# A graph transformer layer on one core: the second half of each item's token products moves behind the next item's slice logits

## What is computed

```
h  = xn @ W.T + b;  a1 = h @ w_a1 + b_a1;  a2 = h @ w_a2 + b_a2
v  = leaky_relu(a1[row] + a2[col], 0.01)            # one score per edge
att = softmax of v over the edges of one row
gnn = segment_sum(att * h[col], row)
mix = linear attention (8 heads, feature map elu + 1) of xn, then @ wo + bo
x   = x + gnn + mix
y   = layernorm(x)
w   = softmax(((y @ W_x + b_x) @ W_slice + b_slice) / temperature)   # 8 heads x 64 slices per node
slice_token = sum over nodes of w * (y @ W_fx + b_fx), over the sum of w
x   = x + (attention among the 64 slice tokens of a head, spread back by w) @ W_out + b_out
```

## Time and profile before

| | us |
|---|---|
| median of 3 runs | 2304.6 |
| lowest, highest run | 2302.0, 2306.59 |
| span of the profiled execution (no other time of it is given) | 2306.1 |
| TensorE busy | 1454.6 |
| VectorE busy | 1270.9 |
| GpSimd busy | 1004.7 |
| ScalarE busy | 677.9 |
| mean granted TensorE clock (share of 2.4 GHz) | 0.798 |

### The profile page before, as it was taken

How to read it: one execution, slowest core, us unless ns; L and a number is a source line. 1 busy time by engine, 2 the same in 40 slices (tenths; PEclk the granted TensorE clock), 3 DMA queues, 4 the chain that set the end, 5 groups by cost and what they waited for, 6 DMA issues and landing times. The chain is left out here.

```text
span 2306.1 us, 27679 instructions
## 1 busy us (share of the span) xinstructions
PE 1454.6 (63%) x8420; PEld 1093.9 (47%) x8420; DVE 1270.9 (55%) x4043; ACT 677.9 (29%) x1884; POOL 1004.7 (44%) x1126
## 2 busy tenths in 40 slices
PE   5599995355745655655655656656646547465889
PEld 3477874234534434434434434434434435344667
DVE  8978783154644644644644545545545535445744
ACT  0243441042322322322322323323323323223310
POOL 1167676535445445445345345345344354453000
PEclk8799997577778877778878778778777777787999
DMA  8011213223223223223223222222232232221064
GB/s 178 29 47 48 62 50 90 71 58 88 70 70 87 69 69 86 69 73 84 68 73 83 68 76 80 68 77 79 65 83 77 62 87 68 69 77 55 14 193 153
DMA packets 112593, 177.17 MB, mean 77 GB/s; under 512 B 35998, under 2 KB 84509, under 8 KB 112445
## 3 DMA queue, kind: packets, MB, share of 16 engines
q0 software_dynamic: 43184, 109.96, 18.0%
q1 hardware_dynamic: 52847, 44.64, 7.5%
q10 hardware_dynamic: 16414, 20.81, 2.9%
HBM read 139.68 MB, written 35.65 MB: 76 GB/s over the span
## 5 line engine op out<-in xcount | busy, mean ns | idle before, releaser
L1134 POOL DMA_INDIRECT big<-node_table,rest x825 | 784.9, 951 | 239.9 <-issue 225.9
L1220 PE MATMUL psum<-big 128*125 128x257 f32 x1700 | 399.2, 388 | 39.4 <-DVE big L1757 39.1
L1220 PEld LDWEIGHTS psum<-big 128*125 128x125 f32 x1700 | 316.2, 191 | 93.9 <-DVE big L1757 46.1
L1575 DVE TENSOR_SCALAR rest<-psum,rest 128x125 f32<-128x125 f32 x100 | 30.1, 344 | 594.8 <-remote 554.1
L1239 PE MATMUL psum<-rest 65*125 65x512 bf16 x52 | 34.6, 666 | 488.6 <-ACT big L1376 488.6
L1132 POOL TENSOR_TENSOR rest<-rest 1x1 f32<-1x1 f32 x100 | 18.9, 189 | 693.7 <-PE psum L1220 668.0
L1370 ACT ACTIVATE rest<-big,rest 128x125 f32<-128x125 bf16 x850 | 268.9, 493 | 134.2 <-DVE rest L1705 134.2
L1239 PEld LDWEIGHTS psum<-rest 65*125 65x125 bf16 x52 | 9.2, 176 | 521.2 <-ACT big L1376 521.0
L1376 ACT COPY big<-psum 128x250 f32<-128x250 f32 x52 | 19.1, 367 | 687.1 <-remote 682.5
L1241 PE MATMUL psum<-rest,big 128*125 128x512 f32 x208 | 177.5, 1005 | 0.0
L1757 DVE TENSOR_SCALAR big<-big,rest 128x125 f32<-128x125 bf16 x850 | 169.0, 281 | 0.0
(11 more groups left out here) (430 smaller groups left out, 2786.7 us busy)
## 6 DMA issues: line engine op xcount, KB each, us to landing
big<-node_table,rest POOLq DMA_INDIRECT x825
slice_weights<-rest ACTq DMA_DIRECT2D x51, 252.0 KB
big<-slice_weights SPq DMA_DIRECT2D x50, 252.0 KB, 3.8
node_table<-big SPq DMA_DIRECT2D x50, 126.0 KB
normalised_turned<-big SPq DMA_DIRECT2D x50, 125.0 KB
rest<-normalised_turned SPq DMA_DIRECT2D x50, 125.0 KB
out_dram<-rest ACTq DMA_DIRECT2D x50, 125.0 KB
X<-in_x_dram SPq DMA_DIRECT2D x1, 5600.0 KB
```

The source lines that it names most:

```text
L1134: pool.indirect_dma_start(Gt[:, u, q * TW:(q + 1) * TW], None, table, bass.IndirectOffsetOnAxis(ap=item[:, u, 2 * q:2 * q + 1], axis=0)).t ...
L1220: mm = pe.matmul(bank[bAgg][0:R, 0:D + 1], P[:, u, q, :], Gt[:, at, q * TW:q * TW + D + 1], start=q == 0, stop=q == Q - 1)
```

## The change

In the gather loop `tokens` of a step is cut in two: the first half of y's columns stays where it was, and the second half is issued in the next step, directly behind that step's `logits`, from the y buffer of the item before; `sum_psum` is raised behind it. The very first step has none of a step before it; the final step first does the half of the item before and then its own two halves as before.

```diff
--- before.py
+++ after.py
@@ -1249,12 +1249,15 @@
                                            start=True, stop=True)
                         mm.then_inc(swT_psum, 1)
 
+                    def token_half(c, u, L=L, last=False):
+
+                        return pe.matmul(bank[bSum + c][:, :], y[:, u, c * 128:(c + 1) * 128], L, start=False, stop=last,
+                                         skip_group_check=True)
+
                     def tokens(n, u, L=L, last=False):
 
-                        for c in range(DC):
-                            mm = pe.matmul(bank[bSum + c][:, :], y[:, u, c * 128:(c + 1) * 128], L, start=False, stop=last,
-                                           skip_group_check=True)
-                        mm.then_inc(sum_psum, 1)
+                        token_half(0, u, L, last)
+                        token_half(1, u, L, last).then_inc(sum_psum, 1)
 
                     def queries(m, v, k):
 
@@ -1298,11 +1301,13 @@
                                            stop=c == DC - 1)
                         mm.then_inc(mix_psum, 1)
 
-                    def step(i, j, k, ahead, final=False):
+                    def step(i, j, k, ahead, final=False, first=False):
                         u, n, odd = j % U, 2 * k + j // U, j % 2
                         v, w, nv = (u + 1) % U, (u + 2) % U, n + 1 if u == U - 1 else n
                         spread(i)
                         logits(i)
+                        if not first:
+                            token_half(1, (u - 1) % U).then_inc(sum_psum, 1)
                         norms(i + 1)
                         if ahead:
                             turn(i + 1, v)
@@ -1319,7 +1324,7 @@
                             logits(i + 1, bF2, yT2)
                             tokens(i, u)
                             return
-                        tokens(i, u)
+                        token_half(0, u)
                         if ahead:
                             queries(i + 2, w, nv)
                         mix(i + 1)
@@ -1332,7 +1337,7 @@
                     turn(0, 0)
                     turn_largest(0)
                     for i in range(SURE):
-                        step(i, i % LU, i // LU, True)
+                        step(i, i % LU, i // LU, True, first=i == 0)
                     with pe.Fori(MIN_ROUNDS - 1, more) as k:
                         for j in range(LU):
                             step(LU * k + j, j, k, True)
```

## The result

| | before | after |
|---|---|---|
| median, us (7 runs each; before: the three runs above and four more) | 2302.0 | 2312.24 |
| lowest, highest | 2292.66, 2306.59 | 2311.38, 2314.56 |
| profiled execution, its span | 2306.1 | 2309.7 (time 2311.46) |
| mean granted TensorE clock, profiled execution | 0.798 | 0.793 |

The changed kernel is slower: the ratio of the times is 1.0046, with a 95% interval of 1.003 to 1.0063, or about 10 us. The forecast was 2321, 16.7 us above its base. The chips are called by letters: B, C and D are three different ones. On which chip this pair ran is not on record; it is called A. Its times before (2292.7 to 2306.6 us) do not overlap those of B and D (2279.7 to 2291.5 us), so it is probably a fourth.

The account below looks back on a forecast made before the run. The prediction took a ring of y copy, gather and delayed y transpose signal as the bound. Tail saving 0 plus 16.7 us of delay on 2306.1 gave 2322.8, on the median's scale 2321; range 2302 to 2340.

Parts of the forecast that it names:

- The ring: Gather loop step: y copy to first edge sums' end 10.83 us, marker and gather 20.15, until y transpose seen 3.16.
- the first piece: Gather loop step, from the y copy to the end of the first edge sums (POOL's marker): 10.83 us.
- Two records at 0.86 or 1.71 us: TensorE, directly behind the logits: the two moved matmul records take 0.86 us at full clock, 1.71 at half.
- The wait on VectorE: VectorE's subtraction waits for sum_psum behind the two records, delaying edge sums and gather: 0.78 us at clock 0.50, 16.7 in all.
- 49 windows: The 1.71 us from 4.31 us after each y copy, whose granted clock prices the records; 15 cost nothing.
- TensorE's room: TensorE's 0.84 us wait for VectorE ahead of the edge sums; 1.71 us more would make them 0.87 late.
- The tail worth nothing: TensorE's tail loses two records, 0.86 us a step, worth 0 because the y transpose's signal is used only after the gather.
- Hidden entirely: Rival: the two records last 0.86 us and fit VectorE's 1.18 us; no change, 2304.6 us, up to 2309; chance 0.17.
- Cold everywhere: Rival: the wait on sum_psum holds 0.78 us in nearly every step, 36 us more, 2341 us; chance 0.12.
- The tail counts: Rival: each matmul record in TensorE's tail costs while POOL gathers; two fewer give 50 us less, 2271 us; chance 0.12.

Follow-up runs that it names:

- half_ahead: Changed kernel with the moved half ahead of the logits, not behind them: 2284.87 us, ratio 0.9994 to the kernel before on chip B; 2284.63 us, 0.9987 on D.
- ring_vector_b: Kernel before, with VectorE's marks and first scores under the gather, weighings before the subtraction, ScalarE's transposes copy before its exponential: 2236.62 us (D); as ring_vector 1593.56 us (C).
- both_behind: Changed kernel with both halves of the token products behind the next step's logits, none in the tail: 2339.52 us, ratio 1.0225 to the kernel before, chip B.
- half_severed: Changed kernel, moved product reading constant weights, sum_psum raised by the tail's half, second half of token sum left out: 2283.54 us, ratio 0.9981 to before, chip B.
- narrowing: Changed kernel with the moved half on 256 of its 512 columns, the other 256 left out: 2284.43 us, ratio 0.9989 to the kernel before, chip B.

## Why the prediction was right, point by point

**The ring** held. In nearly every step of the profiles of chips A, B and D the order is copy, marker, gather, copy; the exceptions are the uneven steps from the 40th on, nine steps of half_ahead on chip B and every fourth of ring_vector_b. Undoing the load on the first piece takes the loss away (half_ahead), doubling it raises the loss (both_behind), and shortening that piece shortens the kernel (ring_vector_b).

**Two records at 0.86 or 1.71 us** held: 1.02 us with the last record's end at 2.4 GHz, 1.92 at 1.2 GHz, streaming 0.86 and 1.71 us.

**The wait on VectorE** held in mechanism and size. Forecast 0.78 us at PEclk 0.50, measured 0.89, of which 0.04 was there before (the start stands 6.34 us after the copy, 5.49 in the earlier trace rows); forecast 16.7 us over the loop, measured 18.5 on chip A and 16.1 on chip D. The marker moved by 0.36 and 0.33 us, forecast 0.35. The forecast had spread the cost over 34 of 49 windows with three sizes. On chip A it came in 19 steps nearly whole, and hardly at all in the others: the clock's rise comes back at the same places every four steps there (3.8, 4.0, 6.4 and 5.7 us after the copy in neighbouring steps), so a step is either mostly cold or not at all. That the sum over such other steps comes out the same is in part luck. The Trainium skill, "TensorE: Matmul & The Clock Gate" (The HAM clock gate), has a throttled state as the default that activity releases; the prediction took this rule, alone, to make the move free. The trace agrees with the release and not with a free move: on chip A it came 5.6 to 6.5 us after the copy in half of the steps, too late for two records that begin at 4.3.

**TensorE's room** of 0.84 us shrank as forecast (the edge sums' line waits 32.2 us for VectorE from 400 to 2050 us, and waited 71.1 us there before), but not to nothing: 0.55 us are left in a warm step. That it is the second bound and not a sum with the first is what half_severed shows: 0.64 us in its coldest steps, where both together give 0.85 to 0.89.

**Where the other 6 us are.** The forecast was 16.7 us, the medians give 10.2. By the forecast's own formula and windows, 14.4 us of the 16.7 lie in the first 38 steps and 2.3 in the rest. The first part held: over these 38 steps the markers come later by 13.7 us in sum on chip A and 12.5 on chip D. The rest of the account did not come out the same on both:

| us, profile after less profile before | chip A | chip D |
|---|---|---|
| first 38 steps, copy to copy | +7.9 | +11.8 |
| of this: copy to marker | +13.7 | +12.5 |
| of this: gather | -1.8 | +0.1 |
| of this: gather end to copy | -4.0 | -0.7 |
| 39th to 49th copy | -4.3 | -0.6 |
| first to 49th copy | +3.6 | +11.3 |
| behind the last copy, the 52nd | +7.5 | +7.1 |

**The tail worth nothing** is thus the term in doubt. The forecast said that it would be wrong if the stretch from gather end to copy shrinks. On chip A it shrinks by 0.10 us a step, on chip D by 0.02. But the kernel before alone has 3.17 us there on A and 2.91 on D, and 20.79 and 20.74 us for the gather, so these differences are no larger than those between two profiles of one kernel, and nothing shows that they come from the shorter tail. The gain behind the 38th step, where 2.3 us of cost were forecast, is not explained either. That 0.36 us less 0.15 us a step, times 47, is 10 us would be a match by accident: the profiled executions of chip A differ by only 3.6 us from the first to the 49th copy.

The last row is not the change at all. In both profiles after, 20 us behind the last copy, TensorE runs 17.1 us at 1.2 GHz; in the profiles of the kernel before on A and D it does not, and from the last copy to the end they take 119.3 and 118.7 us, where those after take 126.8 and 125.8. The kernel before on chip C has the same stretch and takes 126.7; half_severed has none and takes 119.8. So one and the same kernel can end either way, and this is worth 7 us. Part of this stretch, 2196 to 2216 us in after and then in before, columns as in the windows above:

```profile
2196.00:2216.00 20.00, 17.96 (x101) 10.75 (x99) 5.49 (x11) 4.74 (x9) 0.00 (x0) 0.66 0.79 223
```

```profile
2196.00:2216.00 20.00, 15.87 (x120) 10.18 (x119) 7.03 (x15) 5.13 (x10) 0.00 (x0) 1.00 0.66 186
```

The first copy, too, is at 473.2 us in before and 466.0 in after, in a place that the change does not touch. So the 6 us between forecast and result are no more than what one execution differs from another; where they went stays open. The base of the forecast, 2304.6 from three runs, was itself 2.6 us above the median of seven.

**The rivals.** Hidden entirely: wrong on A and D as a whole, right in about half of the steps. Cold everywhere: wrong, the clock is 0.50 in 14 of the 49 windows on A and 12 on D, and not in over 40. The tail counts, by a price for each record: the forecast of 50 us less did not come; both_behind takes four records out of the tail and gives nothing back, and severing or narrowing leaves at most 4.3 us of gain. But its premise, that something holds back TensorE's signals while TensorE's next instructions go on starting, is what chips A, B and D show, and where it does not act, on chip C, the tail does count and the change gains 1.2%. The forecast gave no chance to a chip on which the gather is not in the ring.

## What to carry to other kernels

Before moving work, find which stretch sets the length and price the move at the clock that this stretch has, not at the mean: the same two records cost 0 or 0.89 us by the granted clock behind an idle engine. A counter that guards a buffer moves with the instruction that raises it; ask who overwrites the buffer, and put the instruction in front of the dependence (half_ahead) or give the waiting engine other work first (ring_vector). Before reading a difference of a few microseconds off two profiles, look for a stretch that differs where the change does nothing: here one spell of low clock was worth 7 us. Compare two kernels' delays at equal clock, not by their means. Time a change on more than one chip when a wait in the profile has no releaser that the kernel explains.

## What the runs showed that was not expected

**TensorE's signals are held back while GpSimd gathers, on chips A, B and D and not on C.** In after on chip A the y transpose ends at 1046.42 and its copy starts at 1060.18, 13.8 us later; on chip C, in the same code and under a running gather, it is 0.03 us. By the semaphore updates that the trace records, in that step the signal comes 0.01 us behind the end of the last edge sum, 1.9 behind the spread of the inverse, 1.6 behind the largest, and then 13.9 behind the queries, 13.9 behind mix and 13.7 behind the y transpose, all within 2 us of each other once the gather is over; on chip C each of them is 0.01 to 0.02 us. "Perfetto Trace Analysis" of the Trainium skill (Tensor engine instruction) has a matmul's end as an estimate and its semaphore behind PSUM's acknowledgement; it gives room for such a gap, and the runs give its size. With it the kernel takes 2288 to 2302 us, on chip C without it 1613. Why chip C is free of it stays open: nothing was run that could tell.

**The rise of the clock can lock to the loop.** In the changed kernel it returns every four steps on chip A, about 140 us, so that the same two steps of four pay. On chip D the same kernel has it every six steps, and both_behind on chip B every two (6.2 and 4.9 us after the copy). In the kernel before on chip D it drifts through the step instead and comes round after 12 to 14 steps. What sets the number was not tested.
